# A two-layer decoder on one core: router logits with the weights stationary, and a new order around routings and transposes

## The chip, the cores and the metric

The kernel runs on one core of one Trainium2 chip. The metric is device time in microseconds (us) of one execution, median of several runs. The core's engines each work through a queue of their own in program order: PE (matrix products, with PEld the loads of the stationary operand), DVE and ACT (vector and scalar work), POOL (a third elementwise engine, which also issues gathers and scatters), SP (issues most DMAs). They wait for one another by semaphores.

## The reference

1024 tokens (4 examples of 256) with 256 channels pass through two post-norm layers, all in float32. Layer 0 has linear attention, an expert network chosen by token id, and a mixture of 8 experts of width 256 with "golden" weights. Layer 1 has attention inside groups of 32, cross attention to a masked context, and a mixture of 8 experts of width 176 (top 2) with a shared expert. The change touches both routers and the order around them:

```python
inh = jax.nn.sigmoid(x @ Wr / temperature)                      # golden router, 8 experts
in_zone = (inh >= GOLDEN_LOWER) & (inh <= GOLDEN_UPPER)
distance = jnp.abs(inh - GOLDEN_CENTER)
weights = jnp.exp(-distance / 0.1) * in_zone
fb = jnp.exp(-distance / 0.3)                                   # top 2 of it where no expert is in the zone
...
h = silu(x @ Wg[e]) * (x @ Wu[e])                               # each expert, every token
out = out + weights[:, e] * (h @ Wd[e])
```

The second router has the same product, x @ gate_weight.T with 8 experts, then a softmax and its two largest.

## The kernel before

**Precision.** Every float32 operand is split into a high part in a reduced type and the low rest, and a product is three PE products: high x high, high x low, low x high. ACT makes the high parts (a copy into the reduced type), POOL or DVE the low ones (a subtraction).

**Work units.** Tokens are handled in two halves of 512 (four tiles of 128). Everything is a list of steps per engine: PE_ORDER, ACT_ORDER, POOL_ORDER, DVE_ORDER, SP_ORDER. Each engine runs its list in that order and nothing else decides it. A letter and a number is a step of the expert networks: slot s is 128 columns of a hidden layer for 512 tokens. `g` is a slot's gate product and `u` its up product on PE (6 matmuls of 512 columns each), `s` the silu on ACT (L1239), `m` the product silu x up on DVE (L1897, writes hraw), `h` its high part on ACT (L1253), `l` its low part on POOL (L1495), `d` the down product of a unit on PE (`down`, L883 to L885: 24 matmuls of 256 columns for two slots, 12 for a slot of layer 1; it waits for POOL's low parts by `hid_lo`, for the weights' low part by `d_lo`, and for DVE by `acc_done`), `e` and `f` its two halves, `a` the addition of the weighted result on DVE (L1911). `G` and `D` are the high and low parts of the gate/up and down weights (ACT L1271 and L1282, POOL L1501 and L1506). Units 0 to 3 (slots 0 to 7) are the experts by token id, 4 to 19 (slots 8 to 39) the golden experts, half 0 then half 1. `x1.**` is the placed work of the experts by token id.

**Steps with a dot** are the rest. `r0.*` and `r1.*` are the golden routing of half 0 and 1: `.2` transposes the normalised tokens into xT, `.3` is the router's product on PE (L902), the logits on DVE (L1922, L1923) and the sigmoid on ACT (L1305), `.4` the distance and zone on DVE (L1974 to L1931) and the exponentials on ACT (L1308), `.5` to `.7` the top 2 and the weights on DVE. `a0.22` and `a1.22` are the second layer's routing. `e2.*` and `e3.*` are transposes and cross attention of examples 2 and 3: `.1` and `.11` normalise on ACT (L1126), `.2` and `.12` transpose (PE L577, ACT, DVE L1649), `.3` is the score product (L975). `c` is `later_constants` on DVE (L1772 to L1778): the context mask turned into a cap of 128 x 1024 floats, the count of valid positions, and a bias.

**The router's product before** (`route`): for each of the half's four tiles the tile's 128 tokens are stationary and the router's 16 columns move (8 experts, high and low part of the weights), four products a tile, 16 in all, into bank 6 as tokens x 16. DVE adds the two parts of each expert's logit. Step `r1.3` stands on PE between the down steps `d7` and `d8`, `r0.3` between `g8` and `u8`, `a0.22` between `d18` and `d19`, `a1.22` between `g53 u53` and `d31 d32`.

Gates use PSUM bank 0 or 2 by the parity of the slot, and of slots 2 to 7 each waits until DVE has multiplied the slot two before (`hid_mul`).

Of the kernel before, what the change touches and what calls it, by code (L numbers as in the profile page):

```python
# [16 lines left out]
P = 128  # L17
# [6 lines left out]
GS = 32  # L24
# [18 lines left out]
CONST_W = P + BLK + GS + 8 + QH  # L43
# [119 lines left out]
e0.2 e1.2 h34 s35 G15 h35 s36 e0.3 e1.3 e0.4 e1.4 h36 s37 h37 s38 e0.6 e1.6 h38 s39 e0.7 e1.7 D15 G16 h39 D16 G17 D17
G18 a0.22 s40 D18 e2.11 e3.11 e2.12 e3.12 h40 a0.24 s41 S3 a1.4 h41 s42 h42 S4 G19 D19 G20 D20 G21 s43 h43 a1.9 s44
D21 G22 D22 G23 D23 h44 s45 h45 s46 G24 h46 s47 h47 D24 G25 D25 G26 D26 e2.1 s48 e3.1 e2.2 e3.2 h48 s49 e2.3 e3.3 h49
s50 e2.4 e3.4 h50 G27 D27 G28 D28 G29 D29 s51 e2.6 e3.6 h51 s52 e2.7 e3.7 h52 s53 G30 D30 G31 h53 a1.22 s54 D31 G32
D32 G33 D33 h54 a1.24 s55 h55 s56 G34 h56 s57 h57 s58 D34 G35 D35 G36 D36 G37 D37 h58 s59 G38 h59 s60 D38 G39 h60 s61
# [3 lines left out]
p1 p3 p5 p6 p4 X0 X1 X2 X3 n0.0 G0 D0 l0 l1 n1.0 l2 P0 l3 P1 l4 P2 P3 l5 l6 l7 G1 D1 r0.0 r0.1 Q0 Q1 Q2 Q3 l8 l9 G2 D2
G3 l10 l11 l12 r1.0 l13 D3 G4 l14 S0 l15 l16 l17 D4 G5 D5 G6 D6 l18 l19 G7 D7 l20 l21 l22 l23 G8 D8 G9 e0.10 e1.10 v0
# [2100 lines left out]
```

## Time and profile before

| | |
|---|---|
| median of 3 runs | 423.63 us (422.75, 423.63, 424.76) |
| the profiled execution | 423.83 us, span 421.8 us |
| PE busy | 406.5 us, 96% of the span |
| PEld, POOL, DVE, ACT busy | 84%, 65%, 58%, 56% |
| clock granted to PE | 0.999 of full speed over the span |

The span runs from the first to the last instruction, and the execution's time has 2.0 us more around it. In the page's 40 slices PE is at 9 tenths or more in all but the first and the last. Rows of a timeline give the start in us from the span's start, the duration, engine, line, operation, what it writes and reads, the count, and in brackets the idle time ahead of it with what ended that. Neighbouring instructions of one kind are drawn as one row with a count. A row of waits gives the waiting line, what it waited for, then us in total, times, and the longest.

### The profile page before, as it was taken

The numbers are of one execution on the slowest core, as the hardware profiler recorded it, in microseconds if no ns is written. First come the engines' busy times: TensorE is split into PE (matmuls) and PEld (weight loads), VectorE is DVE, ScalarE is ACT, GpSimd is POOL, SyncE is SP. The second block draws the span as 40 slices with busy tenths as digits, with TensorE's granted clock in tenths as the row PEclk, the third lists the DMA queues.
The fourth block names the chain that finished last, engine by engine and source line by source line (L and its number), as shares of the span: only waits on it lengthen the run. The fifth ranks groups of instructions, "written<-read, shape, count | busy, mean of one in ns | idle before, by whom it ended". The sixth has DMA issues, their size and how long they took to land.

```text
span 421.8 us, 9388 instructions
## 1 busy us (share of the span) xinstructions
PE 406.5 (96%) x3615; PEld 353.5 (84%) x3615; DVE 243.6 (58%) x650; ACT 238.2 (56%) x428; POOL 272.1 (65%) x251
## 2 busy tenths in 40 slices
PE   7999999999999999999999999999999999999994
PEld 6888979987889788898788899798788989888983
DVE  5868767644646676447553578555464675443234
ACT  4756573674575665353733867572546756553543
POOL 2644385377789576864866448457658387787863
PEclk9999999999999999999999999999999999999999
DMA  7933212432134213331322103132533341554402
GB/s 242 306 113 123 66 52 87 151 58 82 53 123 124 93 35 124 82 118 51 103 67 76 39 0 114 51 90 64 172 93 104 101 128 50 165 161 151 149 27 99
DMA packets 23239, 43.09 MB, mean 102 GB/s; under 512 B 3051, under 2 KB 10859, under 8 KB 23196
## 3 DMA queue, kind: packets, MB, share of 16 engines
q1 hardware_dynamic: 21708, 40.92, 30.8%
q0 software_dynamic: 768, 1.05, 1.3%
q8 instruction: 29, 0.48, 0.5%
q10 hardware_dynamic: 720, 0.53, 0.4%
q14 instruction: 14, 0.11, 0.1%
HBM read 38.52 MB, written 3.44 MB: 99 GB/s over the span
## 4 chain that ended last, share of the span: by engine, by line
PE 75%; POOL 7%; DVE 5%; ACT 4%; issue 4%; DMA 3%; SPq 2%; POOLq 0%; DVEq 0%; ACTq 0%
PE bank L554 12%; PE bank L555 11%; PE bank L557 11%; PE bank L883 7%; PE bank L885 7%; PE bank L884 7%; PE bank L963 2%; POOL h_lo L1495 2%; POOL x_tok L1452 2%; PE bank L951 1%; DMA q_buf<-x_cols_dram 1%; PE bank L577 1%; PE bank L902 1%; POOL rstd L1425 1%; POOL xs_dram L1446 1%
## 5 line engine op out<-in xcount | busy, mean ns | idle before, releaser
L1495 POOL TENSOR_TENSOR h_lo<-hraw,h_hi 128x512 fp32r<-128x512 f32 x68 | 88.2, 1310 | 58.0 <-ACT h_hi L1253 57.8
L554 PE MATMUL bank<-xT_hi,pk_hi 128*128 128x512 f32 x240 | 96.9, 404 | 0.0
L555 PE MATMUL bank<-xT_hi,pk_lo 128*128 128x512 f32 x240 | 94.7, 395 | 0.9 <-issue 0.9
L1253 ACT ACTIVATE h_hi<-hraw 128x512 fp32r<-128x512 f32 x68 | 42.8, 629 | 63.4 <-DVE hraw L1897 63.3
L1501 POOL TENSOR_TENSOR pk_lo<-pk_raw,pk_hi 128x512 fp32r<-128x512 f32 (+1 forms) x44 | 75.1, 1706 | 1.6 <-ACT pk_hi L1271 1.4
L557 PE MATMUL bank<-xT_lo,pk_hi 128*128 128x512 f32 x240 | 75.5, 396 | 0.0
L1897 DVE TENSOR_TENSOR hraw<-bank,sil 128x512 f32<-128x512 f32 x68 | 46.9, 690 | 47.9 <-PE bank L557 20.0
L883 PE MATMUL bank<-pk_hi,h_hi 128*128 128x256 f32 x240 | 69.1, 288 | 2.1 <-issue 1.0
L885 PE MATMUL bank<-pk_hi,h_lo 128*128 128x256 f32 x240 | 67.8, 282 | 0.0
L884 PE MATMUL bank<-pk_lo,h_hi 128*128 128x256 f32 x240 | 67.8, 282 | 0.0
L1506 POOL TENSOR_TENSOR pk_lo<-pk_raw,pk_hi 128x256 fp32r<-128x256 f32 (+1 forms) x44 | 41.3, 939 | 21.8 <-ACT pk_hi L1282 21.7
L557 PEld LDWEIGHTS bank<-xT_lo,pk_hi 128*128 128x128 f32 x240 | 45.1, 188 | 11.0 <-DVE xT_lo L1659 0.3
L554 PEld LDWEIGHTS bank<-xT_hi,pk_hi 128*128 128x128 f32 x240 | 45.2, 188 | 10.0 <-issue 0.4
L555 PEld LDWEIGHTS bank<-xT_hi,pk_lo 128*128 128x128 f32 x240 | 45.3, 189 | 9.9 <-issue 1.2
L883 PEld LDWEIGHTS bank<-pk_hi,h_hi 128*128 128x128 f32 x240 | 45.8, 191 | 4.6 <-issue 3.6
L884 PEld LDWEIGHTS bank<-pk_lo,h_hi 128*128 128x128 f32 x240 | 45.8, 191 | 0.7
L885 PEld LDWEIGHTS bank<-pk_hi,h_lo 128*128 128x128 f32 x240 | 45.8, 191 | 0.0
L1282 ACT ACTIVATE pk_hi<-pk_raw 128x256 fp32r<-128x256 f32 (+1 forms) x44 | 21.5, 489 | 36.1 <-PE bank L885 36.0
L1271 ACT ACTIVATE pk_hi<-pk_raw 128x512 fp32r<-128x512 f32 (+1 forms) x44 | 34.2, 778 | 8.5 <-DMA pk_raw<-pk_f_dram 4.7
L1911 DVE SCALAR_TENSOR_TENSOR x_tok<-bank,gold,x_tok 128x256 f32<-128x256 f32 x64 | 27.4, 477 | 12.2 <-PE bank L885 12.2
L1425 POOL TENSOR_TENSOR rstd<-var_e,mhalf 128x2 f32<-128x2 f32 (+1 forms) x19 | 15.3, 805 | 28.1 <-DVE var_e L1616 28.1
L1239 ACT ACTIVATE sil<-bank 128x512 f32<-128x512 f32 x46 | 27.0, 588 | 6.1 <-PE bank L557 6.0
(312 smaller groups left out, 793.9 us busy)
## 6 DMA issues: line engine op xcount, KB each, us to landing
pk_raw<-pk_f_dram SPq DMA_DIRECT2D x28, 384.0 KB, 3.2
pk_raw<-pk_f_dram SPq DMA_DIRECT2D x16, 512.0 KB, 3.7
pk_raw<-pk_f_dram SPq DMA_DIRECT2D x16, 256.0 KB, 2.9
kv_buf<-pk_x_dram SPq DMA_DIRECT2D x4, 512.0 KB, 3.5
x_tok<-x_rows_dram SPq DMA_DIRECT2D x1, 1024.0 KB, 9.3
pk_raw<-pk_x_dram SPq DMA_DIRECT2D x4, 256.0 KB, 6.1
brow<-cw_dram SPq DMA_DIRECT2D x4, 256.0 KB, 3.3
cw_late<-cw_dram SPq DMA_DIRECT2D x4, 256.0 KB, 3.7
```

Source lines behind the costliest of these rows:

```text
L554: pe.matmul(o, w(kc)[0], x(kc)[0], start=kc == 0, stop=False)
L555: pe.matmul(o, w(kc)[1], x(kc)[0], start=False, stop=False)
L557: m = pe.matmul(o, w(kc)[0], x(kc)[1], start=False, stop=kc == KC - 1)
L883: pe.matmul(o, hh, vh, start=first, stop=False, skip_group_check=True)
L884: pe.matmul(o, hh, vl, start=False, stop=False, skip_group_check=True)
L885: m_ = pe.matmul(o, hl, vh, start=False, stop=closed and t % 2 == 1 and kc == chunks - 1, skip_group_check=True)
L1253: A(h_hi[:, row, at * 512:(at + 1) * 512], hraw[:, s % 2, :], ACT.Copy).then_inc(sems["hid_hi"], 1)
L1271: A(g_part(kind, i, pk_hi), raw, ACT.Copy).then_inc(sems["g_hi"], 1)
L1495: pool.tensor_tensor(h_lo[:, row, q], hraw[:, s % 2, :], h_hi[:, row, q].bitcast(F32), ALU.subtract).then_inc(sems["hid_lo"], 1)
L1501: pool.tensor_tensor(g_part(kind, i, pk_lo)[:, 0:w], raw_g(kind, i)[0][:, 0:w], g_part(kind, i, pk_hi)[:, 0:w].bitcast(F32), ALU.subtract) ...
L1506: pool.tensor_tensor(d_part(kind, i, pk_lo), raw_d(kind, i)[0], d_part(kind, i, pk_hi).bitcast(F32), ALU.subtract).then_inc(sems["d_lo"], 1)
L1897: TT(hraw[:, r, :], other[:, :], sil[:, r, :], ALU.mult).then_inc(sems["hid_mul"], 1)
```

## The change

- **Router's product.** Now the router's 16 columns are stationary and the half's 512 tokens move: four products (L909 of the changed kernel) into 16 rows of bank 6. ACT copies those 16 x 512 logits to SBUF (`route_copy`, into cwT). Then `route_sums` turns them back to tokens x experts on PE: for each tile one plain float32 product (L917) with the copy's 128 columns stationary over 16 rows, and 8 moving columns of a new constant `same_expert` (1 where the row's number and the column's agree modulo 8), which also adds the two parts. DVE then reads the logits in one operation instead of two (or one copy instead of a reduction). The new steps are `r0.9`, `r1.9`, `a0.28`, `a1.28`, on PE the sums and on ACT the copy. On PE the sums stand a step or half a step behind the product: `g8 r0.3 u8 r0.9`, `r1.3 e8 r1.9 f8`, `a0.22 e19 a0.28 f19`, `a1.22 d31 a1.28 d32`.
- **Constants.** The cap and the bias of `later_constants` move from DVE to ACT (step `c0`, behind `h13`); what is left on DVE (a reduction straight from the mask, and a small operation) stands behind `m16` and no longer behind `m18`. The mask operation of cross attention has a wait for the cap.
- **A bank.** The gate of slot 6 writes bank 1 and so waits no longer for DVE's product of slot 4, but for an early event of the attention (`a0_res`); the placed work `x1.10` waits for the product of slot 6 instead.
- **Order.** PE: `e2.12 u41 e3.12` (was `e2.12 e3.12 u41`), `g49 e3.2` (was `e3.2 g49`). ACT: the routings' sigmoid and exponentials earlier, ahead of `G6 D6 s18` in the second; `e3.1` ahead of `s48`; `s9` and `s11` ahead of the hidden before them. DVE: `a4` ahead of `m13`, the routing's small groups `r0.5` and `r1.4` to `r1.7` earlier by one or two hidden products or later by one. POOL: `l10` ahead of `D2`.

PE at the second routing, before: the end of down step 7, the 16 products, down step 8 (pk_hi, pk_lo are weights, h_hi, h_lo the hidden, rw the router, xT the transposed tokens).

```order
L885 MATMUL bank<-pk_hi,h_lo 128x256
L902 MATMUL bank<-rw,xT_hi 128x16 [waits xt_lo,xt_hi]
L902 MATMUL bank<-rw,xT_lo 128x16
...
L883 MATMUL bank<-pk_hi,h_hi 128x256 [waits acc_done,hid_lo,d_lo]
L884 MATMUL bank<-pk_lo,h_hi 128x256
L885 MATMUL bank<-pk_hi,h_lo 128x256
...
L883 MATMUL bank<-pk_hi,h_hi 128x256 [waits acc_done]
```

The same place after. The order in which a product's two inputs are named says nothing; con holds `same_expert`, cwT the copied logits.

```order
L894 MATMUL bank<-pk_hi,h_lo 128x256
L909 MATMUL bank<-xT_hi,rw 16x512 [waits xt_lo,xt_hi]
L909 MATMUL bank<-xT_lo,rw 16x512
...
L892 MATMUL bank<-pk_hi,h_hi 128x256 [waits acc_done,hid_lo,d_lo]
L893 MATMUL bank<-pk_lo,h_hi 128x256
L894 MATMUL bank<-pk_hi,h_lo 128x256
...
L917 MATMUL bank<-con,cwT 128x8 [waits rt_T]
L917 MATMUL bank<-con,cwT 128x8 x3
L892 MATMUL bank<-pk_hi,h_hi 128x256 [waits acc_done,hid_lo,d_lo]
```

The product has shrunk to four, and what was one down step is now two halves with the four sums between, each half with its own waits; the sums wait for ACT's copy (`rt_T`).

ACT around the silu of slot 48 (L1239), with the normalisations of examples 2 and 3 (L1126), before:

```order
L1282 ACTIVATE pk_hi<-pk_raw 128x256 [waits down_done,raw1_b]
L1126 ACTIVATE x_tok<-x_tok,shift,rstd 128x256 [waits ln_rstd]
L1126 ACTIVATE x_tok<-x_tok,shift,rstd 128x256
L1239 ACTIVATE bank<-bank 128x512 [waits hid_mul,gate_ready]
L1126 ACTIVATE x_tok<-x_tok,shift,rstd 128x256 [waits ln_rstd]
L1126 ACTIVATE x_tok<-x_tok,shift,rstd 128x256
L1120 ACTIVATE xT_hi<-bank 128x2x256 [waits xt_ps] x2
L1253 ACTIVATE h_hi<-hraw 128x512 [waits down_done,hid_mul]
```

And after (L1146, L1259):

```order
L1302 ACTIVATE pk_hi<-pk_raw 128x256 [waits down_done,raw1_b]
L1146 ACTIVATE x_tok<-x_tok,shift,rstd 128x256 [waits ln_rstd]
L1146 ACTIVATE x_tok<-x_tok,shift,rstd 128x256
L1146 ACTIVATE x_tok<-x_tok,shift,rstd 128x256 [waits ln_rstd]
L1146 ACTIVATE x_tok<-x_tok,shift,rstd 128x256
L1259 ACTIVATE bank<-bank 128x512 [waits hid_mul,gate_ready]
L1140 ACTIVATE xT_hi<-bank 128x2x256 [waits xt_ps] x2
L1273 ACTIVATE h_hi<-hraw 128x512 [waits down_done,hid_mul]
```

The second pair of normalisations has passed the silu, whose input and consumers have stayed where they were.

DVE behind the hidden product 18 (first row), before: the constants (L1772 to L1778) and then the distance and zone of the second routing.

```order
L1897 TENSOR_TENSOR hraw<-bank,sil 128x512 [waits up_ready,silu_done,hid_lo]
L1772 CAST cap<-mask_w 128x1024
L1773 TENSOR_REDUCE valid<-cap 128x4 [waits dve_link]
L1774 TENSOR_SCALAR share<-valid 128x8 [waits dve_link]
L1777 TENSOR_SCALAR cap<-cap 128x1024
L1778 TENSOR_SCALAR bk_four<-con,bcol 128x4 [waits dve_link]
L1974 TENSOR_SCALAR bank<-inh 128x32 [waits rt_sig]
L1975 SCALAR_TENSOR_TENSOR dist<-inh,bank 128x32 [waits dve_link]
L1930 TENSOR_SCALAR bank<-inh 128x32 [waits rt_dist]
L1931 SCALAR_TENSOR_TENSOR pick<-inh,bank 128x32 [waits dve_link]
L1897 TENSOR_TENSOR hraw<-bank,sil 128x512 [waits silu_done,up_ready,hid_lo,dve_link]
```

After, the same engine from hidden products 15 and 16 on:

```order
L1932 TENSOR_TENSOR hraw<-bank,sil 128x512 [waits up_ready,silu_done,hid_lo] x2
L1810 TENSOR_REDUCE valid<-mask_w 128x4
L1812 TENSOR_SCALAR share<-valid 128x8 [waits dve_link]
L1932 TENSOR_TENSOR hraw<-bank,sil 128x512 [waits up_ready,silu_done,hid_lo]
...
L1957 TENSOR_SCALAR lg<-bank,temp 128x32 [waits rt_ps]
L2007 TENSOR_SCALAR bank<-inh 128x32 [waits rt_sig]
L2008 SCALAR_TENSOR_TENSOR dist<-inh,bank 128x32 [waits dve_link]
L1963 TENSOR_SCALAR bank<-inh 128x32 [waits rt_dist]
L1964 SCALAR_TENSOR_TENSOR pick<-inh,bank 128x32 [waits dve_link]
...
L1932 TENSOR_TENSOR hraw<-bank,sil 128x512 [waits up_ready,silu_done,hid_lo] x2
```

Two small operations of the constants are left, two hidden products earlier, and the distance and zone follow the logits (L1957) at once, ahead of an addition and of hidden product 18.

The diff, cut to its core (of the order lists only a line of PE's stands here):

```diff
--- before.py
+++ after.py
-g47 a1.41 u47 a1.26 d24 a1.56 d25 d26 d27 g48 u48 e2.2 e3.2 g49 e2.3 e3.3 u49 g50 u50 e2.4 e3.4 d28 d29 e2.5 e3.5 g51
+a1.25 g46 a1.55 u46 a1.11 g47 a1.41 u47 a1.26 d24 a1.56 d25 d26 d27 g48 u48 e2.2 g49 e3.2 e2.3 e3.3 u49 g50 u50 e2.4
...
+
+        def gate_bank(s):
+            return bank[1 if s == S_F0 - 2 else 2 * (s % 2)]
 
...
                         pe.wait_ge(sems["a0_res"], 4)
+                        pe.wait_ge(sems["hid_mul"], S_F0 - 1)
...
+                elif s == S_F0 - 2:
+                    pe.wait_ge(sems["a0_res"], 3)
...
-            def route(n, router, m):
+            def route(n, router):
 
                 h = n % 2
                 wait_x(n)
+                prods = [(x, kc) for kc in range(KC) for x in (xT_hi, xT_lo)]
+                for j, (x, kc) in enumerate(prods):
+                    m = pe.matmul(bank[6][0:2 * E0, :], rw[:, kc, router, :, :], x_half(x, kc, h),
+                                  start=j == 0, stop=j == len(prods) - 1)
+                m.then_inc(sems["rt_T_ps"], 1)
+
+            def route_sums(m):
+
+                pe.wait_ge(sems["rt_T"], m + 1)
                 for t in range(HT):
-                    o = bank[6][:, t * 2 * E0:(t + 1) * 2 * E0]
-                    prods = [(x, kc) for kc in range(KC) for x in (xT_hi, xT_lo)]
-                    for j, (x, kc) in enumerate(prods):
-                        i = pe.matmul(o, x_tile(x, kc, HT * h + t), rw[:, kc, router, :, :],
-                                      start=j == 0, stop=j == len(prods) - 1)
+                    i = pe.matmul(bank[6][:, t * E0:(t + 1) * E0], cwT[0:2 * E0, t * P:(t + 1) * P],
+                                  same_expert[0:2 * E0, :],
+                                  start=True, stop=True)
                 i.then_inc(sems["rt_ps"], 1)
 
...
-                    route(2 + h, 0, h)
+                    route(2 + h, 0)
+                elif i == 9:
+                    route_sums(h)
...
-                    route(8 + h, 1, 2 + h)
+                    route(8 + h, 1)
+                elif i == 28:
+                    route_sums(2 + h)
                 elif i == 24:
...
+            def route_copy(m):
+                act.wait_ge(sems["rt_T_ps"], m + 1)
+                if m == 3:
+                    act.wait_ge(sems["cw_saved"], 16)
+                A(cwT[0:2 * E0, :], bank[6][0:2 * E0, :], ACT.Copy).then_inc(sems["rt_T"], 1)
...
+            def later_constants():
+                act.wait_ge(sems["in_con"], 16)
+                A(cap[:, :, :], mask_w[:, :].bitcast(U8).rearrange("p (b s) -> p b s", b=B), ACT.Copy, bias=NEG_X,
+                  scale=BIG).then_inc(sems["cap_ready"], 1)
+                A(bk_four[:, :], of_four, ACT.Copy, scale=bcol[:, 5:6]).then_inc(sems["bk_ready"], 1)
...
             def later_constants():
-                link(dve.tensor_copy(cap[:, :, :], mask_w[:, :].bitcast(U8).rearrange("p (b s) -> p b s", b=B)))
-                link(dve.tensor_reduce(valid[:, :], cap[:, :, :], axis=AXX, op=ALU.max))
+                link(dve.tensor_reduce(valid[:, :], mask_w[:, :].bitcast(U8).rearrange("p (b s) -> p b s", b=B),
+                                       axis=AXX, op=ALU.max))
                 TS(share[:, :, 1].rearrange("p (b t) -> p b t", b=B), valid[:, :].unsqueeze(2).to_broadcast([P, B, 2]),
                    BIG, None, ALU.mult)
-
-                link(TS(cap[:, :, :], cap[:, :, :], BIG, NEG_X, ALU.mult, ALU.add))
-                TS(bk_four[:, :], of_four, bcol[:, 5:6], None, ALU.mult).then_inc(sems["bk_ready"], 1)
...
             def logits(m, scale_ap):
                 dve.wait_ge(sems["rt_ps"], m + 1)
-                t0 = HT * (m % 2)
-                src = bank[6][:, 0:HT * 2 * E0].rearrange("p (t a e) -> p t e a", t=HT, a=2)
+                q = slice(HT * (m % 2), HT * (m % 2) + HT)
+                src = bank[6][:, 0:HT * E0].rearrange("p (t e) -> p t e", e=E0)
                 if scale_ap is None:
-                    dve.tensor_reduce(lg[:, t0:t0 + HT, :], src, axis=AXX, op=ALU.add).then_inc(sems["rt_lg"], 1)
+                    dve.tensor_copy(lg[:, q, :], src).then_inc(sems["rt_lg"], 1)
                     dve.wait_ge(sems["rt_lg"], m + 1)
                 else:
-                    link(dve.tensor_reduce(lg[:, t0:t0 + HT, :], src, axis=AXX, op=ALU.add))
-                    TS(lg[:, t0:t0 + HT, :], lg[:, t0:t0 + HT, :], scale_ap, None, ALU.mult
-                       ).then_inc(sems["rt_lg"], 1)
+                    TS(lg[:, q, :], src, scale_ap, None, ALU.mult).then_inc(sems["rt_lg"], 1)
...
             def x1_mask(b):
                 t = 2 * (b % 2)
+                dve.wait_ge(sems["cap_ready"], 1)
...
+    con[:, CONST_W - E0:CONST_W] = p[:, None] % E0 == np.arange(E0)[None, :]
```

## Rows read from the trace of the kernel before

**Rows 1.** The page: busy time of the engines, and the queue that fetches instructions.

```profile
PE 406.5 (96%) x3615; PEld 353.5 (84%) x3615; DVE 243.6 (58%) x650; ACT 238.2 (56%) x428; POOL 272.1 (65%) x251
...
q8 instruction: 29, 0.48, 0.5%
```

**Rows 2.** What PE waited for: us in total, times, longest.

```profile
PE bank L883 <- POOL h_lo L1495: 1.2, 2, 0.8
PE bank L577 <- ACT x_tok L1126: 1.0, 2, 0.7
PE bank L883 <- issue: 1.0, 2, 0.5
PE bank L555 <- issue: 0.9, 1, 0.9
PE bank L554 <- DVE hraw L1897: 0.4, 1, 0.4
PE bank L883 <- DVE x_tok L1911: 0.3, 1, 0.3
```

**Rows 3.** Timeline of PE, second routing: start, us long, instruction, [idle before].

```profile
127.57 0.17 PE L902 MATMUL bank<-rw,xT_hi 128*128 128x16 f32 x1
...
129.28 0.36 PE L883 MATMUL bank<-pk_hi,h_hi 128*128 128x256 f32 x1
```

**Rows 4.** Groups of PE by form: small float32 products (busy us, mean ns).

```profile
L963 PE MATMUL bank<-kv_buf,pT 32*32 32x17 f32 x1024 | 11.5, 181 | 0.8 <-issue 0.8
...
L749 PE MATMUL bank<-pT 128*128 128x8 f32 x2 | 0.4, 256 | 0.0
```

**Rows 5.** Timeline of POOL before the third down step.

```profile
61.59 2.54 POOL L1495 TENSOR_TENSOR h_lo<-hraw,h_hi 128x512 fp32r<-128x512 f32 x2
```

**Rows 6.** Timeline of POOL before down step 4.

```profile
93.06 3.13 POOL L1495 TENSOR_TENSOR h_lo<-hraw,h_hi 128x512 fp32r<-128x512 f32 x2
```

**Rows 7.** Timeline of DVE before down step 5.

```profile
108.62 1.66 DVE L1911 SCALAR_TENSOR_TENSOR x_tok<-bank,gold,x_tok 128x256 f32<-128x256 f32 x4
```

**Rows 8.** Timeline of DVE and then POOL before down step 9.

```profile
135.94 0.83 DVE L1772 CAST cap<-mask_w 128x1024 f32<-128x1024 uint8 x1
...
141.32 1.28 POOL L1495 TENSOR_TENSOR h_lo<-hraw,h_hi 128x512 fp32r<-128x512 f32 x1 [3.26 <-ACT h_hi L1253]
```

**Rows 9.** Timeline of DVE before down step 11.

```profile
153.36 0.69 DVE L1897 TENSOR_TENSOR hraw<-bank,sil 128x512 f32<-128x512 f32 x1
```

**Rows 10.** Timeline of POOL at the second routing.

```profile
127.73 1.28 POOL L1506 TENSOR_TENSOR pk_lo<-pk_raw,pk_hi 128x512 fp32r<-128x512 f32 x1
```

**Rows 11.** Timelines after the second routing: ACT, POOL and PE.

```profile
134.45 1.28 ACT L1305 ACT_TABLE_LOAD   x1
...
132.56 2.40 POOL L1501 TENSOR_TENSOR pk_lo<-pk_raw,pk_hi 128x1024 fp32r<-128x1024 f32 x1
...
137.84 0.39 PE L554 MATMUL bank<-xT_hi,pk_hi 128*128 128x512 f32 x1
```

**Rows 12.** Timeline at the third routing, POOL and then PE.

```profile
255.59 1.26 POOL L1495 TENSOR_TENSOR h_lo<-hraw,h_hi 128x512 fp32r<-128x512 f32 x1
...
256.95 0.35 PE L883 MATMUL bank<-pk_hi,h_hi 128*128 128x256 f32 x1
```

**Rows 13.** Timeline of ACT at the transposes of 321 us.

```profile
321.79 0.58 ACT L1239 ACTIVATE bank<-bank 128x512 f32<-128x512 f32 x1
322.30 1.07 ACT L1126 ACTIVATE x_tok<-x_tok,shift,rstd 128x256 f32<-128x256 f32 x2
```

**Rows 14.** Timeline of DVE in the same stretch.

```profile
323.89 1.34 DVE L1649 TENSOR_TENSOR xT_lo<-bank,xT_hi 128x512 fp32r<-128x512 f32 x2
```

**Rows 15.** Timeline of PE in the same stretch.

```profile
324.17 0.39 PE L554 MATMUL bank<-xT_hi,pk_hi 128*128 128x512 f32 x1
324.40 0.40 PE L555 MATMUL bank<-xT_hi,pk_lo 128*128 128x512 f32 x1
...
325.10 0.28 PE L975 MATMUL bank<-xp_hi,xT_hi 128*128 128x256 f32 x1
```

More of the change, by code:

```diff
@@ L42 @@
 QH = 4
-CONST_W = P + BLK + GS + 8 + QH
+CONST_W = P + BLK + GS + 8 + QH + E0
 BZ = GS + 1
@@ L163 @@
[L163 to L167, printed above, removed]
@@ L168 @@
-h61 s62 D39 G40 h62 s63 D40 G41 D41 h63 s64 G42 D42 G43 h64 s65 h65 s66 h66 s67 D43 h67 z0 z1
+x1.31 x1.14 x1.23 x1.06 x1.32 x1.15 x1.24 x1.33 x1.16 x1.25 x1.34 x1.26 x1.35 r0.2 x1.36 s8 r0.9 r0.3 s9 h8 h9 s10
+r0.4 h10 G2 s11 D2 G3 h11 s12 h12 s13 h13 c0 s14 D3 G4 r1.1 h14 s15 S0 D4 G5 h15 s16 h16 s17 r1.2 h17 D5 r1.9 r1.3
+r1.4 G6 D6 s18 h18 s19 h19 G7 s20 D7 h20 s21 h21 s22 G8 h22 s23 h23 D8 G9 D9 s24 h24 s25 e0.11 e1.11 e0.12 e1.12 G10
+h25 s26 h26 s27 S1 D10 a0.4 S2 h27 s28 G11 h28 s29 h29 s30 D11 G12 a0.9 D12 G13 h30 s31 h31 s32 h32 s33 h33 D13 G14
@@ new lines @@
+s34 e0.1 e1.1 D14 e0.2 e1.2 h34 s35 G15 h35 s36 e0.3 e1.3 e0.4 e1.4 h36 s37 h37 s38 e0.6 e1.6 h38 s39 e0.7 e1.7 D15
+G16 h39 a0.28 D16 G17 D17 G18 a0.22 s40 D18 e2.11 e3.11 e2.12 e3.12 h40 a0.24 s41 S3 a1.4 h41 s42 h42 S4 G19 D19 G20
+D20 G21 s43 h43 a1.9 s44 D21 G22 D22 G23 D23 h44 s45 h45 s46 G24 h46 s47 h47 D24 G25 D25 G26 D26 e2.1 e3.1 s48 e2.2
+e3.2 h48 s49 e2.3 e3.3 h49 s50 e2.4 e3.4 h50 G27 D27 G28 D28 G29 D29 s51 e2.6 e3.6 h51 s52 e2.7 e3.7 h52 s53 G30 D30
+G31 h53 a1.28 a1.22 s54 D31 G32 D32 G33 D33 h54 a1.24 s55 h55 s56 G34 h56 s57 h57 s58 D34 G35 D35 G36 D36 G37 D37 h58
@@ L169 @@
+s59 G38 h59 s60 D38 G39 h60 s61 h61 s62 D39 G40 h62 s63 D40 G41 D41 h63 s64 G42 D42 G43 h64 s65 h65 s66 h66 s67 D43
+h67 z0 z1
 """.split()
 POOL_ORDER = """
[L171 to L173 removed]
@@ new lines @@
+l10 D2 G3 l11 l12 r1.0 l13 D3 G4 l14 S0 l15 l16 l17 D4 G5 D5 G6 D6 l18 l19 G7 D7 l20 l21 l22 l23 G8 D8 G9 e0.10 e1.10
+v0 l24 l25 D9 S1 G10 D10 l26 S2 l27 G11 l28 a0.7 a0.8 l29 D11 G12 D12 G13 l30 l31 e0.0 l32 l33 e0.1 D13 G14 e1.0 e1.1
+D14 l34 G15 l35 l36 l37 e0.5 e1.5 l38 D15 l39 G16 D16 G17 D17 G18 e2.10 e3.10 l40 D18 S3 l41 l42 S4 G19 D19 G20 a1.7
+a1.8 l43 D20 G21 D21 G22 D22 G23 D23 l44 l45 e2.0 G24 l46 l47 D24 e3.0 e2.1 e3.1 G25 D25 G26 D26 l48 l49 l50 G27 D27
+G28 e2.5 e3.5 D28 G29 D29 l51 l52 G30 D30 G31 l53 D31 G32 D32 G33 l54 l55 D33 G34 l56 l57 D34 G35 D35 G36 D36 G37 l58
@@ L178 @@
+D37 G38 D38 G39 l59 l60 l61 D39 G40 l62 D40 G41 l63 D41 G42 D42 G43 l64 l65 l66 D43 l67 y0 w0 w1
 """.split()
@@ L262, in decoder_program @@
         iota8 = con[:, P + BLK + GS:P + BLK + GS + 8]
-        of_four = con[:, P + BLK + GS + 8:CONST_W]
+        of_four = con[:, P + BLK + GS + 8:CONST_W - E0]
+        same_expert = con[:, CONST_W - E0:CONST_W]
         zero_r = sb("zero_r", [P, 512], F32R)
@@ L821, in gate @@
             def gate(s):
+                o = gate_bank(s)[:, :]
                 u, c = unit_of(s)
@@ L837, in gate @@
                 width, at = (D, c * P) if u < U_F1 else (P, 0)
-                product(s, bank[2 * (s % 2)][:, :], 0, width, at, first).then_inc(sems["gate_ready"], 1)
+                product(s, o, 0, width, at, first).then_inc(sems["gate_ready"], 1)
             def up(s):
@@ L1237, in silu @@
                     act.wait_ge(sems["x0_mul"], NB)
-                gate = bank[2 * (s % 2)][:, :]
+                gate = gate_bank(s)[:, :]
                 A(gate if weighted_slot(s) else sil[:, s % 2, :], gate, ACT.Silu).then_inc(sems["silu_done"], 1)
@@ L1300, in golden @@
                     norm_apply(2 + h)
+                elif i == 9:
+                    route_copy(h)
                 elif i == 2:
@@ L1358, in attention @@
                         A(sm_pair[:, b, :], sm_pair[:, b, :], ACT.Exp).then_inc(sems["a1_exp"], 1)
+                elif i == 28:
+                    route_copy(2 + h)
                 elif i == 22:
@@ L1394, in _ @@
                     silu(i)
+                elif step[0] == "c":
+                    later_constants()
                 elif step[0] == "h":
@@ L1890, in hidden @@
                 if u < U_F0:
-                    other = bank[2 * (s % 2)]
+                    other = gate_bank(s)
                 else:
```

40 lines of the change are left out of this document (16 added, 24 removed).

## The prediction

> **What bounds the kernel now.** I read the page's busy times first, then what PE waited for, then the timelines around each of those waits and around each place that the change touches. PE is busy 406.5 us of a span of 421.8, every other engine at most 65% [rows 1]: the time is PE's queue, and a term counts only where it makes PE start something later or earlier. What PE waited for is a short list [rows 2]: two down steps for POOL's low part of the hidden (0.4 and 0.8), transposes for ACT's normalised tokens (0.3 and 0.7), two down steps for "issue" (0.5 each), one 512-column product in mid-air for "issue" (0.9), a gate for DVE's hidden product (0.4), a down step for DVE's adds (0.3). That is 4.8 us that an order could win, and no more. A reading note for all of it: the ends of matmuls are modelled. Two products of 512 columns start 0.23 apart, at 324.17 and 324.40, and each is drawn 0.39 to 0.40 long [rows 15], so a real gap is some 0.16 longer than its idle. I price stalls with that.
>
> **The route, part by part.** Before, it is 16 products of 16 moving columns from 127.57, and the next step begins at 129.28 [rows 3]: 1.71 us, 0.107 each. After, four products of 512 columns: 4 x 0.23 = 0.93 [rows 15]. Then the four sums, plain float32 with 8 moving columns, of which each is carried out in two passes. No row shows that product with 16 rows of a stationary operand. The nearest is L749, the same type and the same 8 columns: its 2 records of 256 ns fill 0.4 us [rows 4], so they overlap, and start to start is at most 0.4 - 0.26 = 0.14, at least 0.11 by PE's other small products (0.107 in rows 3). I take 0.11: 8 passes are 0.89. Low end: L963, 1024 products in 11.5 us, 0.011 each [rows 4], so 0.1 in all; it has 32 stationary columns and L749 has 128, as the sums do, so I lean to L749. High end: no overlap, 8 x 0.256 = 2.05. With 0.07 for each change of shape the new route costs 0.93 + 0.89 + 0.14 = 1.96, or 0.2 more than before; with the low end 0.6 less, with the high end 1.4 more.
> The Trainium skill (TensorE: Matmul & The Clock Gate, section "LDWEIGHTS (loading the stationary operand)") speaks against this change: a load of the stationary operand takes time by its columns, about P/1.2 ns, and not by the rows that are contracted. By it the sums' 16 rows buy nothing, and 8 passes are 8 x 107 ns = 0.85 us; by the pace of L963 they would be 0.1. L749 in rows 4 agrees with the page, as an upper bound.
>
> **What that does at the four places.**
> First routing: the 16 products stood between gate and up of slot 8, and down step 4 later waits 0.8 for POOL's two low parts, which end at 96.19 [rows 2, 6]. PE's 0.2 more is in that wait: 0.
> Second routing: before, both halves of down step 8 followed at 129.28. After, the product is done at 127.57 + 0.94 = 128.51, but the first half needs the low part of its weights, which POOL has at 127.73 + 1.28 = 129.01 [rows 10]; before, the product covered that. It starts at 129.1, 0.18 earlier, and the sums put 0.96 ahead of the second half: +0.78.
> Third routing (second layer): step 19 started at 256.95 right behind POOL's low part of the hidden, 255.59 + 1.26 = 256.85 [rows 12]. A shorter product ahead of it gains nothing, and the sums inside it cost their whole 0.96: +0.95.
> Fourth: a whole down step stands between product and sums, nothing waits: +0.2.
> The copy of the turned logits (128 x 512 by 16 rows, on ACT some 0.6 like its other 512-column work, 0.58 in rows 13) has half a down step before the sums ask for it (12 products of 256 columns, at half the 0.23 of rows 15: 1.4); if that cover were gone it would cost up to 0.6 each.
>
> **The moves.**
> Gate of slot 6 (other bank): its wait of 0.4 for DVE [rows 2] goes. Behind it stands down step 2, one of the two that wait for POOL [rows 2]: it needs the low part of slot 5, the first of two from 61.59 (2.54 for both, so 62.86) [rows 5]. POOL's queue is not touched: 0.
> Down step 5 waits 0.3 for the first two of the four adds that DVE begins at 108.62 [rows 2, 7]. They now stand one hidden product earlier: -0.4. The large constant goes from DVE to ACT behind hidden 13 (some 1.3 us there, as an estimate from the 1.04 to 1.07 of ACT's work of that size [rows 13]; no PE step asks for silu 14 before gate 16, three steps on): 0.
> Down step 9 starts 0.5 late [rows 2]. The row says issue; the last thing it needs is POOL's low part of slot 19, 141.32 + 1.28 = 142.60, and that is late because DVE does the constants from 135.94 on, ahead of the hidden product [rows 8]. The constants go to ACT or earlier and the routing's small operations move: -0.66.
> Down step 11, 0.5 late by the same name, hangs on DVE's hidden product 23 at 153.36, behind the last seven operations of the routing, which now come before hidden product 21 [rows 2, 9]: -0.5 of its 0.65, the rest being the next thing that it needs.
> Transposes of example 2 and 3, first layer-two pass (265 us): the up step of slot 41 (6 x 0.23 = 1.4 us) now stands between them, and the wait of 0.3 goes, 0.5 with its modelled end. A projection behind them still asks for the low part of example 3: -0.4.
> The pass at 321 us: on ACT the silu of slot 48 began at 321.79 and the second pair of normalisations at 322.30 [rows 13]. Now the pair comes first and ends 1.07 later than it could start, near 323.25, so the silu is 1.45 late. DVE's product and then its low parts follow: they began at 323.89, the first done 0.67 later at 324.56 [rows 14], now 326.0. PE's score product that reads them stood at 325.10 [rows 15], now 326.1. The wait of 0.7 for ACT goes [rows 2], but lies ahead of this one and gives nothing beyond it: +1.0.
> Sum: 0.78 + 0.95 + 0.2 - 0.4 - 0.66 - 0.5 - 0.4 + 1.0 = +0.97. The profiled execution took 423.83 us, its span 421.8 and 2.0 around it; that is 0.2 above the median of 423.63 and inside the runs shown, so I add to it: **424.8 us**. With the sums at their low end three routings on PE's path give 3 x 0.8 = 2.4 back (422.4), at their high end they take 3 x 1.16 = 3.5 (428.3).
>
> **Rivals.**
> F, faster: the two anchors on POOL and the one on ACT do not bite, since what is freed ahead moves them too. Then the stalls are won whole, 0.45 + 0.66 + 0.65 + 0.5 + 0.85 = 3.1, less three routings at 0.2: 423.83 - 2.5 = 421.3. For it: POOL is busy 65% and has gaps (3.26 before slot 19 [rows 8]). Against it: at 256.95 PE begins 0.1 behind POOL's end [rows 12], and nothing of the change is ahead of that operation on POOL. Chance 0.20.
> I, the instruction stall: the 0.9 of L555 [rows 2] is in the middle of one slot's products, where no semaphore stands; PE's instructions come in fetches (29 on this queue, 0.48 MB, so 16.5 KB each; 2 x 3615 matmuls and loads over 29 are 249 a fetch [rows 1]), and the change takes some matmuls and loads out at each of the two routings ahead of it. If the boundary now falls where PE's queue is full, 0.9 + 0.2 goes: 423.7. Chance 0.13. The Trainium skill (Runtime: NRT & Kernel Launch, section "Instruction fetch mechanics") has such a boundary every 256 instructions and its cost mostly hidden; by it there is nothing to win, but the trace has 0.9 us that no semaphore explains.
> S, slower: the second routing's chain on ACT. Behind the copy stand a table load and the sigmoid, DVE's distance, a second load and the exponentials, all now ahead of the weights of unit 6 and silu 18; a load is 1.28 [rows 11]. With small operations at 0.2 to 0.5 with their hand-over (an estimate), from 131.45 (sums: 128.51 and half a step, and 0.96) I get logits 131.9, sigmoid 132.2, distance 132.8, exponentials 133.8, the weights' high part 134.9, a third load, silu 18 at 137.4. POOL begins the low part (2.40) at 134.9, before at 132.56 [rows 11], and has slot 19's ready at 142.0. PE's gate 20, at 137.84 before [rows 11], would be at 138.6, down step 9 at 142.8: slack 0.8 to 1.2. The point is there: if the sums come 0.8 late (their high end makes it 1.16) or one load cannot start until its operand is ready (1.28), gate 20 and step 9 wait what is over, and the 0.66 above is not won: 424.8 + 0.5 + 0.66 = 426.0, and up to 427.5 with sums that do not overlap. Chance 0.22.
> That the change doesn't do what it says I can nearly exclude, since the new products are there in both routers.
>
> **How the numbers follow.** My forecast 424.8 has 0.45, F (421.3) 0.20, I (423.7) 0.13, S (426.0) 0.22. About 0.5% (2.1 us, 421.5 to 425.75) is what a measurement can tell from no change. F is faster: 0.20. Forecast and I are within: 0.58. S is slower: 0.22. The range: from 421.4, the middle of F, to 426.8, which leaves out the far part of S and the no-overlap end of 428.3, since rows 4 show overlap. The forecast's own range is 423.6 to 425.7.
>
> **What would show it.** The step from the last route product to the first down product at the second routing should be about 0.6, with POOL's low part of the weights ending just ahead; the four sums should stretch over 0.9 us from their first to the next down product; step 19's first product should still start 0.1 behind POOL's low part of the hidden; the waits of steps 5, 9 and 11 should be gone from the list; the silu at 321 us should come after the second pair of normalisations, and PE should show a wait of about 1 us for DVE's low part. I am wrong in the direction of F if that wait or the 0.6 is missing, and in the direction of S if gate 20 waits for silu 18 or POOL's low part of the weights.

## The result and the profile after

The changed kernel takes 427.1 us (median of 20 runs, 423.2 to 428.8), the kernel before 422.9 in the same runs (421.4 to 425.3): ratio 1.0086, 95% interval 1.0069 to 1.0104, so 3.6 us slower (2.9 to 4.4; the two medians themselves lie 4.2 apart). The forecast of 424.8 was short by 2.3, and its sign was right. The measured median lies 0.3 above the upper end of the range, 426.8, though the interval of the ratio, laid on the 423.6 of before, reaches down to 426.5; and the likeliest case, "within 0.5%", did not come. The one profiled execution took 425.41 us, span 423.6: only 1.8 more than the span of before. That is the first thing to explain: the two traces hold half of what the ratio shows.

Waits of PE after, as in [rows 2] (us in total, times, longest):

```profile
PE bank L981 <- issue: 1.6, 2, 1.1
PE bank L892 <- POOL h_lo L1533: 1.5, 2, 1.1
PE bank L559 <- POOL pk_lo L1539: 1.1, 1, 1.1
PE bank L892 <- issue: 0.9, 1, 0.9
...
PE bank L892 <- POOL pk_lo L1544: 0.4, 1, 0.4
PE bank L1088 <- DVE xT_lo L1687: 0.3, 1, 0.3
```

Much of the list of before is gone, and as long a list has come. Gate 6 (0.4, DVE), step 5 (0.3, DVE), steps 9 and 11 (0.5 each) and both waits for ACT's tokens are off it; the two down steps that wait for POOL's low part of the hidden are still there (1.2 before, 1.5 now). New are the waits behind the shortened product (0.4 for POOL's pk_lo, 0.9 named issue), 1.1 for weights at 323 us, 0.3 for a low part at 268 us, and 1.6 in the products of 32 x 32 (L981; L963 of before had 0.8).

The second routing, PE after, to set beside [rows 3]:

```profile
127.08 0.40 PE L909 MATMUL bank<-xT_hi,rw 128*16 128x512 f32 x1
...
127.78 0.40 PE L909 MATMUL bank<-xT_lo,rw 128*16 128x512 f32 x1
128.59 0.38 PE L892 MATMUL bank<-pk_hi,h_hi 128*128 128x256 f32 x1 [0.42 <-POOL pk_lo L1544]
...
130.22 1.05 PE L917 MATMUL bank<-con,cwT 16*128 16x8 f32 x8
131.20 0.38 PE L892 MATMUL bank<-pk_hi,h_hi 128*128 128x256 f32 x1
```

Product 0.93, a wait, half a down step, sums 131.20 - 130.22 = 0.98. The row has 8 records for the four products, so each is carried out in two passes, 0.12 each: L749 of [rows 4] was the right neighbour, L963 the wrong one.

I laid the 3551 matmuls that both kernels have side by side and read where the later one falls behind. The steps of that difference, in us, after less before:

| place | forecast | traces |
|---|---|---|
| gate 6 and step 2 | 0 | -0.62 + 0.57 |
| first routing, to step 4 | 0 | +0.07 |
| step 5 | -0.4 | -0.44 |
| second routing | +0.78 | -0.27 + 1.09 |
| step 9 | -0.66 | -0.58 |
| step 11 | -0.5 | -0.48 |
| stops named issue, 206 to 217 us | 0 | -0.82 |
| third routing | +0.95 | +1.14 |
| transposes and what follows, 265 to 269 us | -0.4 | 0.0 |
| 286 us and stops named issue, 300 to 306 us | 0 | +0.35 + 0.44 |
| 321 us | +1.0 | +1.0 |
| fourth routing | +0.2 | -0.69 + 0.98 |
| sum | +0.97 | +1.75 |

Without the stops (-0.82 and +0.44) the steps come to +2.1, against +0.97.

### The profile page after: what moved, and what is told of

It reads as the page before. It is cut to its first block, busy times and chain, and to the rows that moved or that the text cites. A ratio compares the mean times of both kernels' runs of the same rounds, so it can differ in the third digit from the quotient of the medians.

```text
span 423.6 us, 9362 instructions
## 1 busy us (share of the span) xinstructions
PE 407.6 (96%) x3599; PEld 352.0 (83%) x3599; DVE 239.3 (56%) x645; ACT 241.3 (57%) x434; POOL 272.4 (64%) x251
## 4 chain that ended last, share of the span: by engine, by line
PE 76%; POOL 7%; DVE 4%; ACT 4%; issue 3%; DMA 3%; SPq 1%; POOLq 0%; DVEq 0%
PE bank L559 13%; PE bank L560 12%; PE bank L562 12%; PE bank L892 7%; PE bank L893 6%; PE bank L894 6%; PE bank L981 2%; POOL h_lo L1533 2%; POOL x_tok L1490 1%; PE bank L969 1%; DMA q_buf<-x_cols_dram 1%; PE bank L582 1%; POOL xs_dram L1484 1%; PE bank L951 1%; POOL rstd L1463 1%
## 5 line engine op out<-in xcount | busy, mean ns | idle before, releaser
L1259 ACT ACTIVATE sil<-bank 128x512 f32<-128x512 f32 x46 | 27.1, 589 | 4.7 <-PE bank L562 4.6
```

## Experiments

**The changed kernel again, twice.** No edit.

> The changed kernel itself, to see what of its median is missing from its profiled execution (425.41 against a median of 427.1, before 423.83 against 422.86). Step theory: the profile is a typical run, the ratio to before near 1.004, and PE's waits by name repeat to 0.2 us each. Fetch theory: the waits named issue in mid-product (L981, 1.6 us in two) differ from run to run by 1 to 2 us and carry the spread of 423.2 to 428.8; the ratio is again 1.009.

> The changed kernel once more, on the chip of the next three, for a third trace of its waits named issue and as their comparator. Both theories: 426 to 427; fetch theory: waits in L981 of 1.5 to 2.5 us again, at the same instructions (192 of 256 in PE's records).

Measured 426.22 (ratio 1.0066, 1.0039 to 1.0093; profiled 424.95) and 427.04 (1.0068, 1.0041 to 1.0096; profiled 425.11). So all three traces of the changed kernel come from the quick end of its runs, and the one of before (423.83) from the upper half of its own 20. By their ratios the two repeats are 2.8 and 2.9 us slower than before. In all three traces PE stands still in L981 at the same two instructions, for 0.62, 1.65, 0.58 us from start to start at 210 us and 1.29, 1.02, 1.08 at 305 us; the third has one more, 0.52 at 214. In sum that is 1.9, 2.7 and 2.2 us, and 2.5 in the trace of before (1.35, 0.54, 0.57): on the average of its traces the changed kernel does not stand longer in them than the kernel before. The start differs too: PE reaches the same product at 9.1, 7.9 and 8.3 us, and at 9.2 in before. Counted over all of PE's records (loads, products and those of its sequencer, 7455 in before, which is 257 for each of the 29 fetches of [rows 1]), every stop of this kind, in which PE waits for no semaphore, comes directly behind the 193rd record of a block of 256, the one of before inside a slot's products [rows 2] included.

**The product alone, from both sides.**

```diff
 # old_route: changed kernel, route() as before, no copy, no sums
-                    m = pe.matmul(bank[6][0:2 * E0, :], rw[:, kc, router, :, :], x_half(x, kc, h), ...
+                        i = pe.matmul(o, x_tile(x, kc, HT * h + t), rw[:, kc, router, :, :], ...
 # new_route: kernel before, with the new route() and its copy and sums; lists of before with
+ u8 r0.9 ; e8 r1.9 f8 ; e19 a0.28 f19 ; d31 a1.28 d32
```

> The changed kernel with the router's product as before (16 products of 16 columns, no copy on ACT, no sums), all other moves kept. Step theory: against the changed kernel PE saves +0.82, +1.14 and +0.29 at routings 2 to 4, 2.2 us, and the first stays hidden: 424.9, ratio to before 1.005 if the moves alone lose, below 1.0 if they win what the waits showed (0.44, 0.58, 0.48). Rival: the product costs nothing, since the wait behind it takes its place: 427.

> The kernel before with the new product, copy and sums alone; constants, bank and the order of everything else as before. Step theory: 0 + 0.8 + 1.1 + 0.3 = 2.2 above before, 425.1, ratio 1.005. If the sums were cheap (0.1 each) and the half-step waits harmless: 0.995 to 1.0.

Measured: old product in the new order 421.61 (ratio 0.9964, 0.9938 to 0.9989); new product in the old order 427.21 (1.0097, 1.0062 to 1.0132). So the new product loses about 4 us, in either order (4.3 and 4.1 by the ratios, each within 1.6 either way), and the moves alone win some 1.5. The expectations named 2.2 for the product, just below those intervals; nearly twice as much came. Where it lies in one execution shows in the trace of the product alone, span 425.4. Laid beside before, its routings hold 0.24 + 0.86 + 1.04 + 0.22 = 2.4. The rest is here, PE and then the windows with PE's granted clock:

```profile
209.91 1.23 PE L977 MATMUL bank<-kv_buf,pT 32*32 32x17 f32 x124
212.55 0.29 PE L977 MATMUL bank<-kv_buf,pT 32*32 32x17 f32 x4 [1.41 <-issue]
...
213.36 0.63 PE L559 MATMUL bank<-xT_hi,pk_lo 128*128 128x512 f32 x1
213.79 0.63 PE L558 MATMUL bank<-xT_hi,pk_hi 128*128 128x512 f32 x1
```

```profile
208.00:212.50 4.50, 3.14 (x133) 2.41 (x132) 2.03 (x5) 3.00 (x5) 4.50 (x3) 1.00 0.50 147
212.50:216.00 3.50, 3.45 (x12) 2.74 (x12) 1.28 (x3) 0.90 (x2) 0.95 (x2) 0.51 0.29 92
216.00:218.50 2.50, 2.50 (x135) 1.98 (x134) 0.70 (x2) 0.73 (x2) 1.48 (x2) 1.00 0.02 4
```

(Columns: stretch, its length, busy us and count of PE, PEld, DVE, ACT, POOL, granted clock, DMA share, GB/s.) After a stop of 1.41 us among the 32 x 32 products PE's granted clock is 0.51, that is 1.2 of 2.4 GHz, for 3.4 us; products of 512 columns then start 0.43 apart and not 0.23, which costs 1.5. The stops named issue in mid-product are 1.0 us longer in sum than before's (3.5 against 2.5). 2.4 + 1.0 + 1.5, less 0.9 by which this run's first wait ended sooner and 0.4 in small steps, is the difference of the spans, 3.6. This is one execution: four of the six timed runs of the product alone have a mean clock of 0.996 or more, against 0.995 here, and still take 426.0 to 428.3 us. The changed kernel's three traces do not have the fall, but 13 of its 37 timed runs have a mean clock of 0.994 or less, and those are 1.7 us longer than its others; of 72 runs of before 7 have it. That is 0.6 us of the changed kernel's mean and 0.2 of before's, so 0.4 of the difference. That the low mean is this fall in them too I infer from the two traces that have it (this and the last experiment, 0.995 and 0.994); the other twelve traces have 0.995 to 0.999, all of it lost at the end of the span, where PE has no work left.

Nor do the stops tell the old product from the new one in the traces: their sum is 2.4 in old_route and 1.9, 2.7, 2.2 in the changed kernel. The spans of old_route and the changed kernel differ by 4.0, of which 1.3 is the start.

**The order at 321 us.**

```diff
-e2.1 e3.1 s48 e2.2        # ACT        -u48 e2.2 g49 e3.2 e2.3    # PE
+e2.1 s48 e3.1 e2.2                     +u48 e2.2 e3.2 g49 e2.3
```

> The changed kernel with silu 48 ahead of the second pair of normalisations on ACT again and the transposes of example 3 ahead of gate 49 on PE again. Step theory: PE's score product comes 1.0 us earlier, 426.1, ratio to the changed kernel 0.9975. Rival: POOL's low part of gate 49's weights (ends 323.91 in the changed kernel) holds PE there anyway, and less than 0.3 comes back.

Measured 424.93 (ratio 1.0056, 1.0032 to 1.008), against 1.0066 for the changed kernel on the same chip: no difference that the intervals can tell. In the trace the silu is early again (322.44 and not 323.73), and PE's score product at most 0.4 earlier by the same measure, not 1.0. The rival's number was right. In the changed kernel gate 49 stood here:

```profile
322.50 0.20 POOL L1464 TENSOR_TENSOR shift<-minus_mean,rstd 128x2 f32<-128x2 f32 x1
322.65 1.26 POOL L1539 TENSOR_TENSOR pk_lo<-pk_raw,pk_hi 128x512 fp32r<-128x512 f32 x1
```

```profile
323.97 0.50 PE L559 MATMUL bank<-xT_hi,pk_hi 128*128 128x512 f32 x1 [1.08 <-POOL pk_lo L1539]
...
326.55 0.36 PE L993 MATMUL bank<-xp_hi,xT_hi 128*128 128x256 f32 x1 [0.49 <-issue]
```

POOL makes the gate's low weights only behind the example's mean and deviation, at 323.91. Moving the gate ahead of the transposes exchanged one wait for the other. But the wait that ends last ahead of the score product L993 is the one that was forecast. It reads DVE's low part, which comes so late because the silu does; this row ends at 326.45, and PE goes on at 326.55, though its row says issue:

```profile
325.77 0.68 DVE L1687 TENSOR_TENSOR xT_lo<-bank,xT_hi 128x512 fp32r<-128x512 f32 x1
```

In the old order DVE is done at 325.23, and nearly the same time passes in another way: PE waits 0.66 for ACT's second pair and comes to the gate at 324.27, 0.2 behind POOL's low weights (324.07), and to the score product at 325.77. Two chains of nearly one length end here, so taking back the late silu gives little.

**Both undone.** The edits of old_route and act31 together.

> The changed kernel with the router's product as before and, besides, silu 48 and the transposes of example 3 in their old order: only the moves that won are left. If the two effects add: 0.9964 to before from the old product and 0.003 from the old order at 321 us, so 0.993, 420.3. If POOL holds PE at 321 us anyway in this one: 0.996.

Measured 421.31 (0.9955, 0.993 to 0.998): the product's gain, and 0.3 from the order in the medians, which the intervals cannot tell from nothing, as in the last experiment.

**The position of PE's instructions among their fetches.** Tiny products shift everything behind them. I took them at 0.011 us each, as L963 [rows 4].

```diff
+            for _ in range(PAD):     # pad48, pad88, both_pad36: at the start, with WARM 8, 7, 8 for 9
+                pe.matmul(bank[3][0:GS, 0:16], zero_r[0:GS, 0:GS], zero_r[0:GS, 0:16], start=True, stop=True)
 # dpad48, both_dpad36: the same into bank 4, in front of down step 4's wait for POOL
```

> The changed kernel with 48 tiny products (32 x 32 stationary, 16 moving) in the idle start and one warm-up product less: nothing else, but every later PE instruction sits 94 places later among its fetches. Fetch theory: the waits named issue in L981's products (2.3 and 1.6 us in two traces) go, the clock never falls at 210 to 216 us, median 424.0 to 424.5, spread down to that of before. Rival (the spread and the missing 1.7 us are the route's own, or DMA's): nothing changes but up to 0.3 at the start, 426.5.

> As the one with 48, with 88 tiny products and two warm-up products less (172 places): the control. Fetch theory: a fetch takes some 2.9 us from boundary to boundary, and here two boundaries fall in short products at 219 us (1.5 us of wait) instead of 210: as slow as the changed kernel or slower, 426 to 427.5. Rival (the padding helps by being there, or hurts by its own time): the same as with 48.

> The kernel with the old product and old order at 321 us, with 36 tiny products at the start (70 places). Fetch theory: its wait in a product of 512 columns at 204 us (1.4) and in L978 (0.7) goes too, 418.5 to 419. Rival: the same as without.

> The changed kernel with 48 tiny products (32 x 32 stationary, 16 moving) in front of down step 4, where PE waits 0.6 us for POOL anyway; the start is untouched, every PE instruction behind 95 us sits 96 places later among its fetches. Fetch theory: the waits in L981 (1.6 to 2.6 us) and what follows them in the clock go: 424.0 to 424.5, 2 to 2.5 below the changed kernel. Rival (the padding at the start lost by the start alone, and the fetches are worth nothing in the median): as the changed kernel, or 0.3 above it.

> Old product, old order at 321 us, and 36 tiny products in front of down step 4 (72 places). Fetch theory: the waits of 1.4 (a product of 512 columns at 204 us) and 0.7 to 1.4 (L978) go: 419.0 to 419.5, ratio 0.990 to before. Rival: 421.3 as without.

| kernel | median | ratio to before | 95% |
|---|---|---|---|
| changed + 48 at the start | 426.27 | 1.0045 | 1.0015 to 1.0075 |
| changed + 88 at the start | 431.06 | 1.0169 | 1.0132 to 1.0207 |
| changed + 48 at step 4 | 426.27 | 1.0040 | 1.0011 to 1.0069 |
| both undone + 36 at the start | 420.96 | 0.9932 | 0.9906 to 0.9957 |
| both undone + 36 at step 4 | 420.28 | 0.9912 | 0.9879 to 0.9945 |

The stops moved much as foretold. With 48 those among the 32 x 32 products sank from 1.6 us of wait to 0.2 and 0.3; at step 4 one of 0.6 came in a gate's product at 306 us. With 88 the longest stands near where it was expected (219 us in the old count, 223.8 in this later trace), in the product of 512 columns behind the short ones, and is longer than expected:

```profile
226.22 0.40 PE L560 MATMUL bank<-xT_hi,pk_hi 128*128 128x512 f32 x1 [2.38 <-issue]
```

But the medians followed only in part, and the rivals named them at least as well: 426.27 twice, where the fetch theory had 424.0 to 424.5 and the rivals 426.5 and "as the changed kernel" (427.04 on that chip). The 88 were 3.6 above the range given for them, and the 36 at the start came to 420.96, against 418.5 to 419 and the rival's 421.3. With 48 products at step 4, on one chip with the changed kernel, 0.8 us came back (ratio 1.0040 against 1.0068, intervals that overlap), not 2.0 to 2.5. The trace shows one reason: the tiny products started 0.032 us apart and not 0.011, so 48 took 1.5 us in a wait of 0.6, and paid 0.9 for stops that fell from 2.2 us (three, start to start, in the third trace of the changed kernel) to 1.2. The padding at the start had a price of its own: in two of those traces (88, and 36) the clock reached its upper level only 13 us into the span and not at 5 to 8. So the theory is right on where PE can stop. What the place is worth is less clear: 88 cost 4.8 us more than 48 in the medians, and their two traces, 9.0 apart, have 4.2 of it in the start and 4.6 in the stops. Nor is it shown that stops make the changed kernel slow: of its 3.6 us the first trace holds 1.8 and the clock some 0.4, and 1.4 have no place in any of them.

The pair with both edits undone shows the same: by the ratios (0.9955, 0.9932, 0.9912) a gain of 1.0 and 1.8 us, with intervals that overlap. The one at step 4 comes nearest to its expectation (0.990): its stops are 0.85 us in sum against 3.3 without the products, its span 2.7 shorter.

**Sums behind a whole step.**

```diff
-r1.3 e8 r1.9 f8      -a0.22 e19 a0.28 f19
+r1.3 d8 r1.9         +a0.22 d19 a0.28
```

> The changed kernel with down steps 8 and 19 whole and the four sums behind them. Step theory: the sums still stand on PE's path (0.9 each), and the product still waits for POOL behind it, so nothing comes back: 426 to 427, if anything 0.3 above for the later logits (silu 18 and the low part of slot 19 come 1.4 us later, past their slack of 0.8). Rival (the half step is what costs, by ACT's copy): 424.5.

Measured 429.99 (1.0134, 1.0104 to 1.0164): 3 us worse than the changed kernel, where I had allowed 0.3. Part of it is the edge that my slower rival spoke of. PE and POOL at down step 9:

```profile
142.39 0.36 PE L892 MATMUL bank<-pk_hi,h_hi 128*128 128x256 f32 x1 [0.28 <-issue]
```

```profile
141.00 1.29 POOL L1533 TENSOR_TENSOR h_lo<-hraw,h_hi 128x512 fp32r<-128x512 f32 x1 [0.63 <-ACT h_hi L1273]
```

Logits 1.4 later put the weights of unit 6 and slot 19's low part later; it ends at 142.29, and step 9 falls 0.7 behind. At the third routing DVE has the logits 2.2 us later than in the changed kernel's trace (260.43 against 258.24), its additions and statistics follow them, and the transposes at 266 us wait for ACT's tokens, 1.3 us:

```profile
265.96 0.84 PE L582 MATMUL bank<-con,x_tok 128*128 128x128 f32 x4 [1.19 <-ACT x_tok L1146]
```

The rest is stops and clock, as in the product alone. The stop in L981 near 210 us is 1.0 longer than in the first trace of the changed kernel, and the one at 308 us (305.65 there) has grown to 2.00, with the clock behind it at 0.52 again, 1.4 us in all:

```profile
309.50:313.00 3.50, 3.50 (x71) 2.52 (x70) 2.05 (x5) 1.66 (x3) 1.32 (x2) 0.52 0.18 42
```

## Why the prediction held in most of its steps and not in its size

**The route.** 1.96 us were forecast for product and sums against 1.71; 0.93 + 0.98 was measured, and 0.1 for each change of shape, for which the forecast took 0.07 without a row. At the second routing the half step started when POOL's low weights were there, 127.26 + 1.28 = 128.54, PE at 128.59, as the forecast had it (0.1 after POOL). +0.82 against +0.78. Right.

**The third routing.** Right in size (+1.14 against +0.95), wrong in one word. I took POOL's end at 256.85 for a fixed time. But PE came 1.4 us earlier, and so did POOL, whose work follows PE's:

```profile
254.18 1.27 POOL L1533 TENSOR_TENSOR h_lo<-hraw,h_hi 128x512 fp32r<-128x512 f32 x1
```

```profile
254.29 0.40 PE L909 MATMUL bank<-xT_lo,rw 128*16 128x512 f32 x1
255.55 0.35 PE L892 MATMUL bank<-pk_hi,h_hi 128*128 128x256 f32 x1 [0.86 <-issue]
```

PE still starts 0.1 behind POOL, at 255.55 and not at 256.95: earlier gains were kept, and only the product's own gain was lost. The row says issue; it was POOL's low part. To that extent rival F was right that POOL's end moves with what is freed ahead of it.

**The moves.** Steps 5, 9 and 11 came within 0.1 of the forecast, and gate 6 gave back at step 2 what it won, for the reason given. Step 265 us failed: the wait for ACT went (-0.5), and 0.5 came back at L1088, which waits for DVE's low part of example 3. I had left 0.1 for that. At 286 us I had nothing, and PE now waits for DVE's mask operation (L2051): +0.35. At 321 us the number was right and so was the chain (silu, DVE, score product), but it is not worth what it costs: the old order has a second chain of nearly the same length, through ACT's tokens and POOL's low weights, and undoing the move returned 0.4 at most.

**The rivals.** S's chain fits to 0.7 us in its places, and this trace ran 0.7 earlier than before's there: exponentials 133.1 to 133.5 (forecast 133.8), silu 18 at 136.26 to 136.86 (137.4), step 9 not waiting; it needed logits 1.4 us later, and had them in the last experiment. The 131.45 from which the forecast laid it out is the sum of 129.1, half a step and 0.96, not of 128.51. I, the stops for instructions, was put at +0 or -1.1 and given 0.13. The 0.9 in L555 did go, and stops among the 32 x 32 products took its place.

**The failed step.** The sum of the steps was too small, +0.97 against +2.1. Its mis-sized terms are the transposes at 265 us (-0.4, measured 0.0), the one at 286 us that it had at nothing (+0.35), and the third routing (+0.95, measured +1.14); the rest is 0.1 or less each. Above that, **I let the product change count for what PE does in its own steps, and put everything elsewhere, stops and clock, at nothing.** The runs show that the product alone costs about 4 us, of which its steps hold 2.4. In its one trace 1.0 is longer stops at fetch boundaries and 1.5 the clock at 1.2 GHz behind such a stop. That does not carry over as it stands: in the changed kernel's own traces the stops are on average no longer than in before's (1.9, 2.7 and 2.2 against 2.5), and its clock explains some 0.4. So of 3.6 us the steps account for 2.1 and the clock for 0.4, and the cause of the last 1.1 us (1.4, since the stops of its first trace were 0.4 shorter than before's) stays open; stops that differ from run to run (by 1.0 at one instruction in its three traces) and the start (by 1.3) are candidates that no experiment separates.

The Trainium skill (Runtime: NRT & Kernel Launch, section "Instruction fetch mechanics") calls the crossing of a 256-instruction block mostly hidden. Here it is hidden at most of the 29 crossings, and not always at those among or just behind the 32 x 32 products: each of the stops, 0.4 to 2.6 us from start to start, two or so in a trace, stands where the 256 records ahead had gone by in 1.1 to 4.4 us.

**The base.** I added to one profiled execution, 0.2 above the median of the three runs shown. With 72 more runs its median was 423.3 to 424.4 on these chips, but in the 20 of the result it was 422.86, 1.0 below my base. So a forecast of +0.97 came out only 2.3 below a time that is 3.6 above before: the base hid part of the miss, and that was luck. The traces of after are from the quick end of its runs, so that they agree with the forecast better than its runs do.

## What to carry to other kernels

Where the engine that bounds the time is full, price a rearranged product by the passes of its small parts: 16 rows instead of 128 saved nothing, and four plain float32 products of 8 columns cost as much as four of 512. A shorter step in front of a wait gives nothing if the other engine's end is set by something else, and a step placed between two halves costs its whole length. And count instructions, not only time: a change of a few dozen can move a fetch boundary into a run of very short products, where PE stopped here, and in two traces the clock fell behind such a stop. If a change's gain is below 1%, try it with the old order and the new, and shift it by some dozen tiny instructions, before judging it; and do not take a trace of each kernel for the difference of their medians, which here was twice as large.

The best version that I ran is none of the two: the product as before, the moves kept except at 321 us, and 36 tiny products in front of down step 4, 420.28 us (ratio 0.9912, 0.9879 to 0.9945). Its interval overlaps those of the same kernel without the tiny products and with them at the start, so that only the step from before to these three is shown.

## What the runs showed of the hardware that was not expected

- PE's stops of 0.4 us or more for which no semaphore was late, 32 in 14 traces and all behind 200 us, lie at one place of a block of 256, directly behind the 193rd of all PE's records (loads, products and the sequencer's). They are 0.4 to 2.6 us from start to start, in or just behind runs of 128 products of 32 x 32 that take 1.2 us. Rows named issue elsewhere, such as 0.86 at 255 us (POOL) and 0.49 at 326 us (DVE) in the changed kernel, were waits for another engine.
- After a stop of 1.4 us (and of 2.0 in the last experiment) among such products the granted clock was 0.51 to 0.52 for 3.4 us, although PE was busy 3.45 of 3.50 us then. It is no fixed rule: after a stop of 1.5 in the second trace of the changed kernel, of 1.4 in the last experiment, and of 2.4 in the one with 88, it stayed at 1.00.
- In two traces with tiny products at the start (88, and 36) the granted clock reached 1.00 at 13 us instead of 5 to 8; with 48 there it did so at 5.5. The record of the clock begins there, and the mean clock of a span does not count what is ahead of it.
